# Lag attention: the odd output part is added by VectorE from the bank of the queries' spectra, ScalarE turns a sign, and routing opens with four wide products

## The reference, cut to what matters

```python
# layer 1 (8 heads, C = 2), Q = layernorm(x), K = V = ctx
qf = jnp.fft.fft(q, axis=2); kf = jnp.fft.fft(k, axis=2)
corr = jnp.fft.ifft(qf * jnp.conj(kf), axis=2).real
topk = int(C * np.log(L))                       # 11 of 256 lags, for every channel
w, idx = jax.lax.top_k(corr.transpose(0, 1, 3, 2), topk)
w = jax.nn.softmax(w, axis=-1)
for i in range(topk):                           # a weighted sum of shifted copies of v
    g = jnp.minimum(idx[:, :, None, :, i] + pos, L - 1)
    out = out + w[:, :, None, :, i] * jnp.take_along_axis(v, g, axis=2)
x = x + jnp.tanh(g_xattn[0]) * out
# layer 2: experts; the router works on layernorm(x)
logits = x @ gate_w.T; probs = softmax(logits); vals, idx = top_k(probs, 2)
x = x + jnp.tanh(g_ffn[0]) * experts(layernorm(x))
# layer 3: attention to ctx; layer 4: quantised feed-forward
```

## Time and profile before

| | us |
|---|---|
| median of three runs | 1365.92 |
| the profiled execution, its own time | 1363.27 |
| its span, first to last instruction | 1361.5 |
| busy in the span: PE, DVE, ACT, POOL | 1213.9, 794.3, 511.1, 617.4 |
| `lag_attention`, up to the barrier | 0 to 426.2 |
| `route`, opening | 426.2 to 431.1 |

### The profile page before, as it was taken

How to read it: one execution, slowest core, us unless ns; L and a number is a source line. 1 busy time by engine, 2 the same in 40 slices (tenths; PEclk the granted TensorE clock), 3 DMA queues, 4 the chain that set the end, 5 groups by cost and what they waited for, 6 DMA issues and landing times. The chain is left out here.

```text
span 1361.5 us, 20741 instructions
## 1 busy us (share of the span) xinstructions
PE 1213.9 (89%) x6364; PEld 836.0 (61%) x6370; DVE 794.3 (58%) x2009; ACT 511.1 (38%) x891; POOL 617.4 (45%) x996
## 2 busy tenths in 40 slices
PE   4798888889867999999999998999999999768776
PEld 2344444445435854468878876989888889435443
DVE  3889999998973680025433332543555443468885
ACT  2545454454424400024222221332222232078884
POOL 5788889898753001023212122323321221168885
PEclk8999999999978899999999998999999999879998
DMA  5220212302004503127778864536323330121111
GB/s 193 86 70 31 92 62 93 140 31 109 0 1 160 212 1 110 42 93 269 270 230 275 274 227 142 183 98 159 101 83 119 124 94 32 63 69 58 50 62 78
DMA packets 52480, 156.10 MB, mean 115 GB/s; under 512 B 5952, under 2 KB 16192, under 8 KB 52416
## 3 DMA queue, kind: packets, MB, share of 16 engines
q1 hardware_dynamic: 39152, 113.33, 23.5%
q0 software_dynamic: 13264, 41.95, 10.8%
HBM read 112.80 MB, written 45.61 MB: 116 GB/s over the span
## 5 line engine op out<-in xcount | busy, mean ns | idle before, releaser
L1216 PEld LDWEIGHTS ex_bank<-ex_xT,ex_gu 128*112 128x112 f32 x1248 | 140.4, 177 | 24.6 <-issue 23.7
L1216 PE MATMUL ex_bank<-ex_xT,ex_gu 128*112 128x128 f32 x1248 | 143.7, 273 | 2.4 <-issue 1.5
L44 PE MATMUL xa_bank<-fT_high,M_hi 128*128 128x256 f32 x512 | 143.8, 281 | 0.0
L46 PE MATMUL xa_bank<-fT_high,M_lo 128*128 128x256 f32 x512 | 142.8, 279 | 0.0
L45 PE MATMUL xa_bank<-fT_low,M_hi 128*128 128x256 f32 x512 | 142.8, 279 | 0.0
L1080 POOL TENSOR_TENSOR ex_small<-listed,ex_small 128x1 int32<-128x1 int32 x42 | 15.4, 366 | 225.1 <-DVE Wk L1158 225.0
L44 PEld LDWEIGHTS xa_bank<-fT_high,M_hi 128*128 128x128 f32 x512 | 96.5, 188 | 0.3
L46 PEld LDWEIGHTS xa_bank<-fT_high,M_lo 128*128 128x128 f32 x512 | 96.5, 188 | 0.0
L45 PEld LDWEIGHTS xa_bank<-fT_low,M_hi 128*128 128x128 f32 x512 | 96.1, 188 | 0.0
L297 POOL TENSOR_TENSOR la_osum<-la_oprod 128x512 f32<-128x512 f32 x64 | 80.2, 1273 | 35.0 <-DVE la_oprod L501 35.0
L52 PE MATMUL la_bank<-la_tab,la_cross 128*128 128x256 f32 x256 | 65.5, 413 | 32.2 <-POOL la_cross L290 29.5
(11 more groups left out here) (283 smaller groups left out, 2848.5 us busy)
## 6 DMA issues: line engine op xcount, KB each, us to landing
produced<-Wk SPq DMA_DIRECT2D x39, 512.0 KB
ex_gu<-in_gate_up SPq DMA_DIRECT2D x16, 896.0 KB
X<-in_x SPq DMA_DIRECT2D x8, 1024.0 KB, 7.2
la_v_raw<-in_ctx SPq DMA_DIRECT2D x16, 512.0 KB, 4.0
produced<-la_zeros SPq DMA_DIRECT2D x16, 512.0 KB, 4.7
normal<-rt_xn SPq DMA_DIRECT2D x16, 512.0 KB, 5.7
fT<-in_ctx_T SPq DMA_DIRECT2D x8, 1024.0 KB, 5.7
xa_f<-in_ctx SPq DMA_DIRECT2D x8, 1024.0 KB, 4.9
```

The lines of the kernel that those rows point to most:

```text
L44: pe.matmul(out, a[0], b[0], start=first, stop=False)
L46: return pe.matmul(out, a[1], b[0], start=False, stop=last)
L1216: m = pe.matmul(bank[half][0:INTER, 0:P], gu[:, slot, at:at + INTER], xT[:, k, :], start=(k == 0), stop=(k == KD - 1))
```

## The change: who adds the odd part, who turns the sign, and how routing opens

The odd part no longer goes through ACT and POOL. `positions(u, 1)` writes it into bank 1, that of the queries' spectra, and DVE adds it from there, one step later, between the second and the third list, with the gate or its negative as the factor. PE's product of the queries' odd half into bank 1 waits for that (`added1`). The tile `odd`, ACT's `odd_rows` and POOL's `add_odd` are gone. The largest value's sign is turned by ACT, ahead of each exponential, and DVE writes a spare column in its place. In `route` PE starts with four products of 512 columns into bank 7, whose results nothing reads, and the wait for the later constants moves to `sums`.

```diff
+        part_bank = [bank[4], bank[1]]
...
-            def add_odd(u, b, h):
-                pool.wait_ge(s["odd_out"], u + 1)
-                for j in range(2):
-                    pool.wait_ge(s[f"added{j}"], u + 1)
-                    xs = X[:, bass.ds(2 * b + j, 1), halfsl(h)].rearrange("p o c -> p (o c)")
-                    pool.tensor_tensor(xs, xs, odd[:], ALU.add if j == 0 else ALU.subtract).then_inc(s["odd_added"], 1)
...
-                if before2:
-                    add_odd(*before2)
...
+            act.activation(less_tg[:], tg[:], ACT.Copy, scale=-1.0).then_inc(s["less_gate"], 1)
...
             def exponent(u, c):
-                at_least(act, s["maxed"], 4 * u + c + 1)
+                at_least(act, s["top_chain"], 20 * u + 5 * c + 1)
+                act.activation(neg_max[:, c:c + 1], top[:, c, 0:1], ACT.Copy, scale=-1.0).then_inc(s["negated"], 1)
                 at_least(act, s["wtr"], u)
+                at_least(act, s["negated"], 4 * u + c + 1)
                 act.activation(wt[:, c, :], corr[:, c, :], ACT.Exp, bias=neg_max[:, c:c + 1]).then_inc(s["exed"], 1)
...
-            def odd_rows(u):
-                at_least(act, s["out_pe"], 2 * u + 2)
-                at_least(act, s["odd_added"], 2 * u)
-                act.activation(odd[:], bank[5][:], ACT.Identity, scale=tg[:, 0:1]).then_inc(s["odd_out"], 1)
...
             dve.wait_ge(s["tgd"], 1)
+            dve.wait_ge(s["less_gate"], 1)
...
                 for c in range(4):
+                    if c == 2:
+                        earlier()
                     at_least(dve, s["corr_sb"], 2 * u + c // 2 + 1)
...
-                    dve.tensor_scalar(neg_max[:, c:c + 1], top[:, c, 0:1], -1.0, None, ALU.mult).then_inc(s["maxed"], 1)
+                    dve.memset(spare[:], 0.0)
...
-            def add(u, b, h, j):
-                at_least(dve, s["out_pe"], 2 * u + 1)
-                xs = X[:, bass.ds(2 * b + j, 1), halfsl(h)]
-                dve.scalar_tensor_tensor(out=xs, in0=bank[4][:].rearrange("p (a c) -> p a c", a=1), scalar=tg[:, 0:1], in1=xs,
-                                         op0=ALU.mult, op1=ALU.add).then_inc(s[f"added{j}"], 1)
+            def add(u, b, h, part):
+                at_least(dve, s["out_pe"], 2 * u + part + 1)
+                if part:
+                    at_least(dve, s["added0"], 2 * u + 2)
+                for j in range(2):
+                    xs = X[:, bass.ds(2 * b + j, 1), halfsl(h)]
+                    factor = less_tg if part and j else tg
+                    dve.scalar_tensor_tensor(out=xs, in0=part_bank[part][:].rearrange("p (a c) -> p a c", a=1), scalar=factor[:, 0:1], in1=xs,
+                                             op0=ALU.mult, op1=ALU.add).then_inc(s[f"added{part}"], 1)
...
+                def odd_part():
+                    if before2:
+                        add(*before2, 1)
...
                 full_product(pe, bank[0][:], rows_t(0), q_n[:, 0, :])
+                at_least(pe, s["added1"], 2 * (u - 2))
                 full_product(pe, bank[1][:], rows_t(1), q_less[:]).then_inc(s["spec_q"], 1)
...
-                at_least(pe, s["added1"], u)
+                at_least(pe, s["added0"], 2 * u)
                 full_product(pe, bank[4][:], lags_t(0), more, True, False)
                 full_product(pe, bank[4][:], last_t(2), less, False, True)
-                at_least(pe, s["odd_out"], u)
...
+WIDE = 4
...
         def _(pe):
-            pe.wait_ge(s["consts"], 3)
+            pe.wait_ge(s["consts"], 1)
...
             def sums():
+                pe.wait_ge(s["consts"], 3)
...
+            for i in range(WIDE):
+                full_product(pe, bank[7][:], X[:, 0, 0:P], X[:, 0, 0:512])
             for t in range(2):
                 pe.wait_ge(s["xn_ready"], t + 1)
```

More of the change, by code:

```diff
@@ L141, in lag_attention @@
         osum = sb("osum", [P, 4, C])
-        odd = sb("odd", [P, C])
         v_less = sb("v_less", [P, 2, C])
@@ L146, in lag_attention @@
         tg = sb("tg", [P, 1])
+        less_tg = sb("less_tg", [P, 1])
         graw = sb("graw", [P, 1])
@@ L391, in weights_out @@
                     act.activation(wT[:, j, :], bank[6 + j][:], ACT.Copy).then_inc(s["wt_ready"], 1)
-            def odd_rows(u):
-                at_least(act, s["out_pe"], 2 * u + 2)
-                at_least(act, s["odd_added"], 2 * u)
-                act.activation(odd[:], bank[5][:], ACT.Identity, scale=tg[:, 0:1]).then_inc(s["odd_out"], 1)
             def step(on, due):
-                before, now, after, next2 = on(-1), on(0), on(1), on(2)
+                now, after, next2 = on(0), on(1), on(2)
                 if now:
@@ L422, in step @@
                     weights_out(now[0])
-                if before:
-                    odd_rows(before[0])
             steps(act, step)
@@ L445, in c_products, with top_lags @@
                     dve.tensor_tensor(prod[:, i, :], bank[qk][:], v_spectrum(u, vk), ALU.mult).then_inc(s["prods"], 1)
-            def top_lags(u, between):
+            def top_lags(u, earlier, between):
                 def finish(c, part):
@@ L502, in o_products, with lags @@
                                           ALU.mult).then_inc(s["oprods"], 1)
-            def add(u, b, h, j):
-                at_least(dve, s["out_pe"], 2 * u + 1)
-                xs = X[:, bass.ds(2 * b + j, 1), halfsl(h)]
-                dve.scalar_tensor_tensor(out=xs, in0=bank[4][:].rearrange("p (a c) -> p a c", a=1), scalar=tg[:, 0:1], in1=xs,
-                                         op0=ALU.mult, op1=ALU.add).then_inc(s[f"added{j}"], 1)
-            def lags(u, between):
+            def add(u, b, h, part):
[7 more added lines that the diff above has]
+                                             op0=ALU.mult, op1=ALU.add).then_inc(s[f"added{part}"], 1)
+            def lags(u, earlier, between):
                 for name, each in PER_UNIT.items():
                     counted[name], counted["base " + name] = 0, u * each
-                top_lags(u, between)
+                top_lags(u, earlier, between)
                 assert all(counted[name] == each for name, each in PER_UNIT.items()), counted
@@ L524, in step @@
                 if now:
-                    lags(now[0], products)
+                    lags(now[0], odd_part, products)
                 else:
+                    odd_part()
                     products()
@@ L529, in step @@
                     add(*before, 0)
-                    add(*before, 1)
                 if before2 and before2[2] == 1 and not (isinstance(before2[1], int) and before2[1] == B - 1):
-                    at_least(dve, s["odd_added"], 2 * before2[0] + 2)
+                    at_least(dve, s["added0"], 2 * before2[0] + 2)
+                    at_least(dve, s["added1"], 2 * before2[0] + 2)
                     scales_after.variance(dve, X, before2[1])
@@ L597, in positions @@
                 at_least(pe, s["osums"], 4 * u + 2 * j + 2)
-                full_product(pe, bank[4 + j][:], pos_t(KINDS[2 * j]), osum[:, 2 * j, :], True, False)
-                full_product(pe, bank[4 + j][:], pos_t(KINDS[2 * j + 1]), osum[:, 2 * j + 1, :], False, True).then_inc(s["out_pe"], 1)
+                full_product(pe, part_bank[j][:], pos_t(KINDS[2 * j]), osum[:, 2 * j, :], True, False)
+                full_product(pe, part_bank[j][:], pos_t(KINDS[2 * j + 1]), osum[:, 2 * j + 1, :], False, True).then_inc(s["out_pe"], 1)
             def step(on, due):
```

4 lines of the change are left out of this document (2 added, 2 removed).

## The result

The changed kernel takes 1378.68 us (median of four runs, 1376.64 to 1381.6) and the kernel before, in runs of the same session, 1365.94 (1365.62 to 1366.14). The ratio is 1.0095, its 95% interval 1.0076 to 1.0114: slower, by 12.7 us in the medians. The profiled execution took 1377.94 us with a span of 1376.2, against 1363.27 and 1361.5. The forecast was 1380.7 for the median and 1378 for the profiled execution.

A forecast was written before the change was run, and what follows sets the result against it. DVE was taken to bound the middle units, its busy time hiding a wait. Added to the profiled 1363.27 us, the terms summed to +14.8 us: 1378 us profiled, 1380.7 us median, range 1367 to 1389.

The forecast's parts named there:

- rival (a): Loop: POOL, not DVE, sets the pace, so the moved additions fill DVE's waits for it; 1362 us; chance 0.10.
- The pairs, +1.33 us each: DVE between lists 1 and 2: each added pair of odd-part additions delays what follows by 1.33 us; 14 make +18.6 us.
- The third list's product, -6.4 over 14 units: DVE, third list's masked product: no longer stretched once POOL is idle there; surplus over 0.43 us in eight units, -6.4 us.
- The sign on ACT, +4.8 over 14 units: List 3: exponential 0.25 us later, so the masked product loses the race to POOL's fold in eight units; +4.8 us.
- The sign on DVE, -1.4: DVE, about two lists a unit: a spare write replaces the sign instruction, saving 0.05 us 28 times; -1.4 us.
- List 0, -3.3 in units 2 and 15: Before list 0: DVE waits less for ACT without the odd rows, 1.3 us each, plus 0.66 in unit 15; -3.3 us.
- The clock in the loop, +1.5: PE in the loop: longer waits for POOL's sums bring half-clock correlations in more units, mostly in PE's slack; +1.5 us.
- Start and tail, +0.25 and -1.8: Start: DVE's first statistics wait for one more ACT operation, +0.25 us; loop's end: one DVE pair replaces ACT's and POOL's work, -1.8.
- The wide products, +2.5: Routing's opening on PE: four products run two at half clock, two at full, then transposes at full; +2.5 us.
- (b): Whole change: edits cancel if the late exponential loses no race and the replaced sign gives 9.6 us; 1367.7 us; chance 0.10.
- (c): Loop: PE becomes the bound through half-clock stretches in nearly every unit, +11.7 in place of +1.5; 1391 us; chance 0.12.
- (d): PE's product of the queries' odd half waits for DVE's pair, delaying everything behind; 1385 us; chance 0.08 with another rival.

The follow-up runs named there:

- the first four experiments: Changed kernel without wide products, 1376.37 us; kernel before with only wide products, 1365.92 us; with only the sign on ACT, ratio 1.0028; with only the odd part on DVE, 1373.66 us.

## Why the prediction was right, and where its sizes were not

**The bound.** The step stands where the change acts. From the end of list 0's product to that of list 3's, 16.24 of the 23.84 us, DVE never waited long in the kernel before: its idle time there is 1.06 us in the mean, in gaps that hardly ever reach 0.3 us, while POOL idles 2.65. The pairs and the products of lists 1 to 3 lie in this part, so they are paid for in full; POOL's work fell by 39 us (617.4 to 578.0 with the odd part alone) while the unit grew from 23.84 to 24.55. In the rest of the unit, from list 3's product to the end of list 0's, it is POOL that sets the end, as rival (a) had noted. Before, in nine of the twelve middle units:

```profile
218.06 1.26 POOL L273 TENSOR_TENSOR la_q_n<-la_q_n 128x512 f32<-128x512 f32 x1
...
218.75 0.85 DVE L456 SCALAR_TENSOR_TENSOR la_wt<-la_rest,la_wt 128x256 f32<-128x256 f32 x1
```

The product ends at 219.60, 0.28 us behind POOL's fold, and POOL had folded without a pause since 212.87, when ACT gave it the last list's weights. With the change a fold sets the end in all twelve. From product to product it is 7.54 to 7.57 us in every such unit, in the kernel before and in the changed one, but for unit 13 of the latter. So in that part DVE gains nothing by being early, but it does when the product is put behind other work, as the delayed one showed.

**The pairs, +1.33 us each.** 1.32 in the experiment with the odd part alone; 15.8 us over the twelve units.

**The third list's product, -6.4 over 14 units.** All eight long ones lie in the twelve middle units, where the mean falls from 0.97 to 0.42, -6.6. The mechanism is that of the forecast, POOL's two additions gone, and so is the size.

**The sign on ACT, +4.8 over 14 units.** The race is lost in 14 of 14, as forecast; wait and longer product cost 0.20 + 0.18 = 0.38 us a unit, +4.6 over twelve, where seven of the eight short products make +4.2 by the forecast. A lost race costs its 0.2 us of wait also where the product had been long already, but the product then takes 0.85 us and not 1.03. The experiments with the sign alone and with list 3's sign back on DVE both show it by itself. The race is nearer than the text of the forecast has it: in the kernel before the product is long where POOL's fold starts within 0.03 us of it, as in the unit of the earlier trace rows, and short where the fold starts 0.06 to 0.09 us behind it. Then it is POOL that is held:

```profile
234.62 0.42 DVE L456 SCALAR_TENSOR_TENSOR la_wt<-la_rest,la_wt 128x256 f32<-128x256 f32 x1
...
234.69 0.94 POOL L282 TENSOR_TENSOR la_wt<-la_wt 128x254 f32<-128x254 f32 x1
```

The same fold took 0.72 us at 211.03.

**The sign on DVE, -1.4.** The stretches to products 1 and 2 shorten by 0.06 and 0.05 us, product 1 by 0.02: -1.6 over twelve. Forecast -1.2 for as many.

**List 0, -3.3 in units 2 and 15.** From the end of list 3's product to that of the next unit's list 0, unit 2 gave -1.2 and unit 15 -3.4, where 1.3 and 2.0 were forecast. In unit 15 some 1.7 us of it can't be put down to the odd rows: DVE had been idle for 1.77 us ahead of the maximum, behind the correlations that ran at half clock (376.34, 5.39 us) and at full clock in the changed kernel. With the sign alone they ran at full clock too (382.83, 3.72 us), and the stretch took 7.57 us in place of 9.28. In the middle units the three rows fall from 7.60 to 7.44, -1.9 in all, and no term was set for this. Of it 1.2 us are unit 13's, which is of the same kind as 2 and 15, without statistics between the steps, and has no term in the forecast; before and after:

```profile
337.27 1.02 DVE L456 SCALAR_TENSOR_TENSOR la_wt<-la_rest,la_wt 128x256 f32<-128x256 f32 x1 [2.78 <-ACT la_wt L380]
```

```profile
347.32 0.86 DVE L443 SCALAR_TENSOR_TENSOR la_wt<-la_rest,la_wt 128x256 f32<-128x256 f32 x1 [1.95 <-ACT la_wt L374]
```

With the odd part alone unit 13 gave nothing (7.56 us): its product started later and met POOL's last fold. The other 0.6 us come from units 4, 6 and 12, where the exponential behind the odd rows, and not POOL, had released list 0's product.

The five terms give 15.8 - 6.6 + 4.6 - 1.6 - 1.9 = 10.3; the twelve units grew by 10.43. The forecast's terms give 16.0 - 6.4 + 4.2 - 1.2 + 1.3 = 13.9 for them, the last being the clock; that is 25.0 us a unit, where it named 24.9.

**The clock in the loop, +1.5.** In the twelve units it cost nothing; where half clock did reach DVE, in unit 15 before, it is the changed kernel that was spared. The correlations at half clock went from 4 to 5 of 13, not to "more units", the wait for the sums from 2.20 to 2.45 us, not to 3.6: the pause didn't grow by what DVE adds. Nor does the wait decide which correlations are slow: the slow ones stood behind 1.92 to 3.02 us, the fast ones behind 1.88 to 3.11. From one correlation's start to the next, units behind a slow one took 24.74, 24.99, 24.75, 24.96 and 24.75 us, the others 23.49 to 24.98. And the mean clock fell by 0.01 only (0.98 to 0.97 over 90 to 390 us).

**Start and tail, +0.25 and -1.8.** DVE's first statistics moved from 10.25 to 10.53, +0.28. From list 3 of unit 15 to the start of routing it is -2.2. Routing starts 8.6 us later in all, not the 12 to 15 that the forecast named as its sign.

**The wide products, +2.5.** Here the forecast was mis-sized; +4.1 in the changed kernel, +3.3 alone. The step that failed was "The clock rose as those transposes ended. If it rises after as much work now, two products stand at half, two at full". In the changed kernel PE worked from 435.38 to past 441 at the lower level, in the kernel without these products from 436.08 to the same moment, and before from 427.61 to 431. So the time that PE worked ahead of the rise differs from case to case, from 3.4 to about 5.7 us, and the wide products did not move the rise in either pair; what sets its moment no run here shows. All they did was to put their own length, nearly all of it at half clock, ahead of the transposes, and to let these fall behind the rise. The bound of +6 held. In the medians the edit shows as 2.3 us, by the two ratios as 1.4; alone it costs 0 to 0.39% of the time.

**What stays open.** The last 2.0 us. From the first instruction of the experts' stage to the end it took 830.3 us in the changed kernel and 828.3 before, and 824.7 to 832.2 in the first four experiments, where no instruction of these stages was touched. The remainder is smaller than this scatter, and no run was made to find what sets it.

**The rivals.** (a) would have needed the pairs to fill waits for POOL; they lengthened the unit in both pairs of kernels that differ by them, since POOL's hold on the path lies in another part of the unit. (b) needed the race not to be lost and the sign to give 0.15 us each; it gave 0.06. (c) is out by the unit lengths above, (d) by the 2.3 to 3.8 us between the pair and PE's product that waits for it. The forecast's sum of +14.8 came so near the +14.7 measured by luck, through errors that cancel: 3.5 too much in the loop's twelve units (1.9 for list 0, 1.3 for the clock), 1.6 too little at the opening, and the 2.0 left open.

## What to carry to other kernels

Before moving work off an engine, ask whether that engine's busy time or its interference is what the path pays: here 2.5 us a unit came off POOL, of which the path felt 0.55, and 1.33 went onto DVE, in a part of the unit where it sets the pace. Interference is cheaper taken away by order: one masked product put behind two instructions that POOL doesn't hold up gave 13 us, of which list 0's own rows account for the larger part. An operation of 0.2 us ahead of a critical one costs more than its length when the critical one had won a race by 0.06 us: here 0.2 of wait and 0.43 of longer product.

## What the runs showed of the hardware

The hold between DVE and POOL depends on the form of DVE's instruction. A two-input product on 128 x 256 in SBUF takes 0.42 us free and, begun within a POOL fold or addition, up to 1.53 us: it then ends 0.28 us behind it. Additions of 128 x 512 with one input in PSUM (1.41 us for two), the maximum (0.42) and the strike-out (0.41) are not stretched. Where the product starts 0.06 us ahead, POOL's fold takes 0.94 us in place of 0.72.

How near such a race runs was unexpected: before the change list 3's product was long in six of 14 units, with 0.02 or 0.03 us between its start and that of POOL's fold, short in eight, with 0.06 to 0.09, and 0.22 us more on ACT made it long in all.

Work put ahead of PE's transposes did not raise its clock earlier: it went to the upper level at 431 with the wide products (begun at 426.84) and without them (transposes begun at 427.61), and just after 441 with them (435.38) and without (436.08).
